# A state-space block and an attention block on one core: order of work around the second head pair, and a fourth padded buffer

## The reference, cut to what matters

```python
x = x + _L0_conv_ref(_gn(x), ...)          # block 0: selective scan
# block 1, on v = _gn(x)
qkv = einsum('bchw,oc->bohw', v, w_qkv) + b_qkv
qkv = conv3x3_depthwise(qkv, w_dw) + b_dw
q, k, v = split(qkv); q, k, v -> (b, 4 heads, 48, 2304)
q = q / max(sqrt(sum_channels(q * q)), 1e-12); k likewise
attn = softmax(einsum('bhdn,bhdm->bhnm', q, k) * temperature)
out = einsum('bhnm,bhdm->bhdn', attn, v)
x = x + einsum('bchw,oc->bohw', out, w_proj) + b_proj
```

## Time and profile before

| what | value |
|---|---|
| median of 3 runs | 15295.29 us |
| the profiled execution's own time | 15298.41 us |
| its span (first to last instruction) | 15296.6 us |
| mean granted clock of TensorE | 0.968 of full |
| TensorE matmul busy | 86% of the span |
| VectorE / ScalarE / GpSimd busy | 84% / 72% / 69% |

### The profile page before, as it was taken

How to read it: one execution, slowest core, us unless ns; L and a number is a source line. 1 busy time by engine, 2 the same in 40 slices (tenths; PEclk the granted TensorE clock), 3 DMA queues, 4 the chain that set the end, 5 groups by cost and what they waited for, 6 DMA issues and landing times.

```text
span 15296.6 us, 237874 instructions
## 1 busy us (share of the span) xinstructions
PE 13084.6 (86%) x60888; PEld 7840.4 (51%) x60888; DVE 12871.7 (84%) x13813; ACT 11081.7 (72%) x22746; POOL 10502.7 (69%) x4158
## 2 busy tenths in 40 slices
PE   6888888889888888888988889888898888988889
PEld 4555455554555545555455554555445554455544
DVE  8999669996799857998589984899849998499984
ACT  5887578875788657886578866788667886678865
POOL 6998069980699707997079960899608995099950
PEclk9999999999999999999999999999999999999999
DMA  3433023430334303342034420334203342044420
GB/s 111 129 129 114 20 93 129 138 96 20 97 129 138 92 20 103 129 138 87 20 111 129 136 80 20 115 129 136 75 20 120 129 135 71 20 129 129 132 65 25
DMA packets 907942, 1467.94 MB, mean 96 GB/s; under 512 B 38912, under 2 KB 891904, under 8 KB 893664
## 3 DMA queue, kind: packets, MB, share of 16 engines
q1 hardware_dynamic: 906560, 1452.37, 29.9%
HBM read 1350.07 MB, written 102.17 MB: 95 GB/s over the span
## 4 chain that ended last, share of the span: by engine, by line
PE 31%; issue 22%; POOL 19%; DVE 18%; ACT 5%; DMA 4%; DVEq 1%; ACTq 0%; POOLq 0%; SPq 0%
POOL area L1490 14%; DVE area L1013 13%; PE ps L838 9%; PE ps L849 8%; POOL area L1500 5%; PE ps L654 4%; DMA area<-bc_rows 4%; DVE area L1031 3%; ACT ps L1294 1%; PE ps L584 1%; PE ps L752 1%; PE ps L729 1%; PE ps L641 1%; ACT ps L1255 1%; PE ps L712 1%
## 5 line engine op out<-in xcount | busy, mean ns | idle before, releaser
L1013 DVE TENSOR_TENSOR_SCAN area<-ps,hst,area 128x384 f32<-128x384 f32 x9216 | 8571.3, 993 | 116.4 <-POOL area L1490 48.8
L1490 POOL TENSOR_TENSOR area<-area 128x1152 f32<-128x1152 f32 x3072 | 8001.9, 2638 | 50.3 <-POOL area L1479 38.1
L1294 ACT ACTIVATE ps<-area,a_neg 128x384 f32<-128x384 f32 x9216 | 5289.3, 580 | 1148.0 <-DVE area L1013 1087.8
L654 PE MATMUL ps<-area,ident 128*128 128x384 f32 x12672 | 4610.8, 501 | 790.4 <-POOL area L1500 722.0
L654 PEld LDWEIGHTS ps<-area,ident 128*128 128x128 f32 x12672 | 2277.6, 193 | 2506.5 <-POOL area L1500 947.2
L1474 POOL TENSOR_TENSOR area<-area,ones 128x2304 f32<-128x2304 f32 x8 | 43.3, 5417 | 3521.5 <-ACT area L1219 3399.9
L641 PE MATMUL ps<-ident,area 128*128 128x128 f32 x17280 | 2420.8, 277 | 5.2 <-ACT area L1263 5.2
L1433 ACT ACTIVATE area<-ps,t_neg,area 128x768 f32<-128x768 f32 x1728 | 1617.7, 986 | 984.6 <-PE ps L838 984.6
L641 PEld LDWEIGHTS ps<-ident,area 128*128 128x128 f32 x17280 | 2195.1, 193 | 58.9 <-ACT area L1263 9.5
L1500 POOL TENSOR_TENSOR area<-area 128x1152 f32<-128x1152 f32 x768 | 2024.8, 2636 | 34.7 <-ACT hst L1239 34.7
L1263 ACT ACTIVATE area<-ps,area 128x384 f32<-128x384 f32 x2880 | 1637.4, 569 | 535.1 <-PE ps L632 531.5
(11 more groups left out here) (128 smaller groups left out, 9606.7 us busy)
## 6 DMA issues: line engine op xcount, KB each, us to landing
area<-bc_rows SPq DMA_DIRECT2D x1536, 768.0 KB, 6.8
xz<-x_normed SPq DMA_DIRECT2D x144, 288.0 KB, 6.3
area<-in_x SPq DMA_DIRECT2D x18, 1728.0 KB, 10.4
area<-x_padded SPq DMA_DIRECT2D x24, 1250.0 KB, 5.6
z_raw<-z_st SPq DMA_DIRECT2D x144, 192.0 KB, 6.2
area<-z_raw SPq DMA_DIRECT2D x8, 3456.0 KB, 15.0
x_padded<-x_st SPq DMA_DIRECT2D x120, 200.0 KB, 7.7
x_normed<-area SPq DMA_DIRECT2D x9, 1728.0 KB, 7.9
```

The lines of the kernel that those rows point to most:

```text
L654: m = e.matmul(ps[:, 5 + j, 0:CH], ident[:], hb[:, i % NH, j], start=i == 0, stop=i == N - 1)
L1013: e.tensor_tensor_scan(rev(hb[:, i % NH, j], k), rev(ps[:, 2 + j, 0:CH], k), rev(dbu[:, i % NH, j], k), hst[:, i, j:j + 1], ALU.mult, ALU. ...
L1294: e.activation(ps[:, 2 + j, 0:CH], dlt[:, par, j], ACT.Exp, scale=a_neg[:, j, k, i:i + 1]).then_inc(da, 1)
L1490: e.tensor_tensor(dbu[:, i % NH], du[:, par], row_b[:, q % 2, i % ROWS:i % ROWS + 1].broadcast_to([128, J, CH]), ALU.mult).then_inc(dbus, 1)
```

## The change

- A fourth padded buffer: `xp2` gets `xpads[1]`, and `PAD_OF` says which buffer a tile takes: tiles 0 to 3 have one each, tile 4 reuses buffer 0, tile 5 buffer 1. `pad_qkv(i)` waits only for i > 3, and then for the convolution of tile i - 4. GpSimd clears the border of a fourth buffer: four more memsets for each image.
- In pair 0, `qkv(3)`, `qkv(4)` and `qkv(5)` each move one place ahead on PE and ACT: tile 3 before the transposes of v, tile 4 before the norms of q, tile 5 directly after them.
- `k_norms` is split in two halves of nine matmuls. In pair 1 the first half goes between `q_norm(1, 3)` and `q_norm(1, 4)`; in pair 0 the halves follow each other.
- On DVE, `scale_q(1)` and `newton_k(1)` go after two divisions of pair 0, ahead of the other four.
- On PE, the wait for six divisions moves from before the first `scores` of pair 1 to before its first `values`.

```diff
--- before.py
+++ after.py
@@ -93,6 +93,7 @@
 WQ = SUMS + 128
 WPR = WQ + CT * QT * 128
 XPAD2 = WPR + PAIRS * C + 4
+PAD_OF = (0, 1, 2, 3, 0, 1)
 UK = 3
 UC = UK * NC
 UNIT_AT = (10, 14)
@@ -194,7 +195,7 @@
         kz = ar(KZ, PAIRS * L).rearrange("p (i l) -> p i l", i=PAIRS)
         v_v = ar(V, PAIRS * L).rearrange("p (i l) -> p i l", i=PAIRS)
         vt = ar(VT, PAIRS * MT * 128).rearrange("p (i m c) -> p i m c", i=PAIRS, m=MT)
-        xp2 = [ar(XP2 + i * PADS, PAD).rearrange("p (h w) -> p h w", h=HP) for i in range(3)]
+        xp2 = [ar(XP2 + i * PADS, PAD).rearrange("p (h w) -> p h w", h=HP) for i in range(3)] + xpads[1:]
         kr = ar(KS, 2 * MT)
         kn = ar(KS + 2 * MT, PAIRS * 2 * MT).rearrange("p (i m) -> p i m", i=PAIRS)
         ksc = ar(KS + 6 * MT, PAIRS * 2 * MT).rearrange("p (i m) -> p i m", i=PAIRS)
@@ -346,7 +347,7 @@
         def conv_qkv(e, b, i):
             p, kind = divmod(i, 3)
             e.wait_ge(qk_ev, b * 36 + (6 * i + 6 + 2))
-            conv_taps(e, b * 108, i, cv2, xp2[i % 3], (v_v[:, p], q_v[:, p], kz[:, p])[kind], w_dw, b_dw)
+            conv_taps(e, b * 108, i, cv2, xp2[PAD_OF[i]], (v_v[:, p], q_v[:, p], kz[:, p])[kind], w_dw, b_dw)
 
         def copy_vt(e, b, p, g):
 
@@ -771,13 +772,14 @@
                     e.matmul(ps[:, c % 2, 0:CH], hones[:], sqq[p][:, c * CH:(c + 1) * CH],
                              start=True, stop=True).then_inc(n_mm, 1)
 
-                def k_norms(p):
+                def k_norms(p, half):
 
                     e.wait_ge(qsq, b * 4 + 2 * p + 2)
-                    for m in range(MT):
+                    for m in range(MT // 2 * half, MT // 2 * (half + 1)):
                         i = e.matmul(ps[:, 2, 2 * m:2 * m + 2], sqk[p][:, m * 128:(m + 1) * 128], hind[:],
                                      start=True, stop=True)
-                    i.then_inc(n_mm, 1)
+                    if half == 1:
+                        i.then_inc(n_mm, 1)
 
                 def row_sum(p, c):
 
@@ -790,15 +792,16 @@
                     if p == 0:
                         for i in range(3):
                             qkv(i)
+                        qkv(3)
                         wait_cv2(e, b, 0)
                         for g in range(5):
                             transpose_v(0, g)
-                        qkv(3)
+                        qkv(4)
                         for c in range(NC):
                             q_norm(0, c)
-                        qkv(4)
                         qkv(5)
-                        k_norms(0)
+                        k_norms(0, 0)
+                        k_norms(0, 1)
                         e.wait_ge(qk_ev, b * 36 + 36 + 2)
                     else:
                         e.wait_ge(ex, (b * 6 + 3) * 36 + 3)
@@ -810,8 +813,10 @@
                                 row_sum(0, 0)
                                 row_sum(0, 1)
                                 group_sum(b * 2 + 3, 1)
+                            if c == 4:
+                                k_norms(1, 0)
                             q_norm(1, c)
-                        k_norms(1)
+                        k_norms(1, 1)
                         row_sum(0, 2)
                         row_sum(0, 3)
                         wait_cv2(e, b, 3)
@@ -820,7 +825,6 @@
                         row_sum(0, 4)
                         row_sum(0, 5)
                         e.wait_ge(gn_v, b * 2 * GN_OPS + 4 * GN_OPS)
-                        e.wait_ge(on, b * 12 + 6)
                     e.wait_ge(vt_ev, b * 10 + (5 * p + 5))
                     e.wait_ge(qn, b * 2 + (p + 1))
                     e.wait_ge(k_ac, b * 6 + (3 * p + 3))
@@ -845,6 +849,9 @@
                             e.wait_ge(ex, base + (w + 4))
                             if w == 0:
                                 e.wait_ge(o_ev, turn + 1)
+                                if p == 1 and c == 0:
+                                    alone(e)
+                                    e.wait_ge(on, b * 12 + 6)
                             for s in range(2):
                                 i = e.matmul(ps[64 * h:64 * h + 64, 6 + s, 0:CH], vt[:, p, m, 64 * h:64 * h + 64],
                                              pb[:, w % 4, s * CH:(s + 1) * CH], start=m == 0, stop=m == MT - 1)
@@ -1122,10 +1129,12 @@
                 e.wait_ge(x_in, b * 32 + 64)
                 channel_stats(xf)
                 groupnorm(b * 2 + 3, 0, xf, xf)
-                for c in range(NC):
-                    divide(0, c)
+                divide(0, 0)
+                divide(0, 1)
                 scale_q(1)
                 newton_k(1)
+                for c in range(2, NC):
+                    divide(0, c)
                 e.wait_ge(n_mm, b * 14 + 14)
                 e.wait_ge(vt_mm, b * 10 + 10)
                 conv_tiles(b + 1)
@@ -1356,13 +1365,13 @@
 
                 def pad_qkv(i):
 
-                    if i >= 3:
-                        wait_cv2(e, b, i - 3)
+                    if i > 3:
+                        wait_cv2(e, b, i - 4)
                     alone(e)
                     with e.Fori(0, 3) as cc:
                         for s in range(2):
                             e.wait_ge(qk_mm, b * 36 + cc * 2 + (6 * i + s + 1))
-                            e.activation(xp2[i % 3][:, ds(cc * 16 + (8 * s + 1), 8), 1:1 + W],
+                            e.activation(xp2[PAD_OF[i]][:, ds(cc * 16 + (8 * s + 1), 8), 1:1 + W],
                                          ps[:, 6 + s, 0:CH].rearrange("p (h w) -> p h w", w=W),
                                          ACT.Identity, bias=b_qkv[:, i:i + 1]).then_inc(qk_ev, 1)
 
@@ -1397,14 +1406,14 @@
                     if p == 0:
                         for i in range(3):
                             pad_qkv(i)
+                        pad_qkv(3)
                         for g in range(5):
                             copy_vt(e, b, 0, g)
-                        pad_qkv(3)
+                        pad_qkv(4)
                         wait_cv2(e, b, 1)
                         e.activation(sqq[0], q_v[:, 0], ACT.Square).then_inc(qsq, 1)
                         for c in range(NC):
                             q_norm(0, c)
-                        pad_qkv(4)
                         pad_qkv(5)
                         k_norms(0)
                     else:
```

## The result

| kernel | median, us | runs |
|---|---|---|
| before | 15294.74 | 15293.58 to 15296.45 (4) |
| changed | 15188.81 | 15186.56 to 15191.55 (4) |

The ratio is 0.9931, 95% interval 0.9918 to 0.9944: 105.9 us faster, where 77 were forecast (15218). The time lies in the range, 4.8 us above its lower end. The profiled execution of the changed kernel has a span of 15187.3 us against 15296.6, and the mean granted clock went from 0.968 to 0.973.

A forecast was written before the change was run, and what follows sets the result against it. Attention's PE-ACT chain, its pair 1 scores held up by `scale_q`, was taken as what to relieve. 3.84 + 4.61 + 0.7 + 0.5 = 9.65 us an image, 77.2 for eight, gave 15218 us; range 15184 to 15250.

The forecast's parts named there:

- Norms in halves: Pair 1, PE: first nine norms of k fill the gap before `q_norm(1, 4)`, what follows moves forward; 3.84 us an image.
- `scale_q` ahead and the wait moved: Pair 1, DVE and PE: first scores no longer wait for `scale_q`, the divisions' wait moves to the values; 4.61 us an image.
- The divisions take it back: Rival, chance 0.13: pair 1's late root of k delays divisions, or the stop moves to the values; 40 us in all, 15255.
- the case of a full clock: Pair 1: were first scores at full clock, 1.4 us less, first values would still have half a microsecond to spare.
- The first scores: Pair 1, PE: first scores at 0.50 clock might run faster without the stop; bounds 0 and 3.1 us, 0.7 taken.
- Pair 0: Tiles one place ahead: norms of k start 3.65 us earlier but probably at half clock; between 0 and 3.65, 0.5 taken.
- HAM oscillation — how this bites in real kernels: Skill's rule: PE waiting between bursts starts the next cold; by it pair 0's term is 0, the kernel at 15222.
- The first rival: Chance 0.14: clock stays up for pair 0's norms and both pairs' first scores; 14.1 us an image, 113 in all, 15182.

The follow-up runs named there:

- scale_only: Kernel before with scale_q and newton_k behind two divisions and the divisions' wait moved to the first values, norms of k whole: 15223.85 us, ratio 0.9955.
- before_warm1: Kernel before with five 128x384 matmuls added on PE in pair 1, in the idle time ahead of the first scores, waits unchanged: 15272.02 us, ratio 0.9986.
- after_warm0: Changed kernel with six 128x384 matmuls added on PE in pair 0, behind tile 5 and ahead of the norms of k: 15180.77 us, ratio 0.9924.
- pad_only: Kernel before with only the fourth padded buffer and the new places of tiles 3 to 5: 15280.84 us, ratio 0.9991.
- wait_back_again: Changed kernel with the wait for six divisions back ahead of pair 1's first scores, measured once more: 15223.70 us, 15200.91 to 15241.44 in 12 executions.
- wait_back: Changed kernel with the wait for six divisions moved back ahead of pair 1's first scores: 15226.67 us, 15200.59 to 15235.58 in four executions.
- warm_mix0: Changed kernel with six matmuls added ahead of pair 0's norms of k and one more behind every fourth norm, four in all: 15209.74 us.

## Why the prediction was right, and where it was off

- **Norms in halves, 3.84 us: right.** 2.07 us for the first half in the gap, `q_norm(1, 4)` not delayed, 3.84 saved behind it. Alone it gave 24.5 us in place of 31 (3.1 an image; 3.5 by the length of attention).
- **`scale_q` ahead and the wait moved, 4.61 us: right.** Together with the halves 8.52 by the trace against 8.45. "The divisions take it back" did not happen: the values had 2.2 us to spare. The prediction had left half a microsecond for the case of a full clock; the last division ends about where it said, 1.9 us after the first score starts, but the values come later, since the second eight scores, which wait for an exponential, stand ahead of them (9353.07).
- **The first scores, 0.7 us: the term that was mis-sized.** It measured 3.42, beyond the bound of 3.1, and makes 22 us of the 29 that the forecast fell short. I had the bounds from the right rows and then took a value near the row of before, because PE "does little from 3716 on". That weighed the wrong stretch: scale_only has the slow norms in it and scores at full clock behind them, before_warm1 shows that filling the stop alone is enough. The edit removes the stop that lowered the clock, and with it the reason to stay near the row of before. The bound was low by 0.3 because I took the steady 2.94 us between the first pairs of exponentials; with a full clock the first two stand 9354.66 - 9352.02 = 2.64 apart.
- **Pair 0, 0.5 us: right in kind, slightly generous.** It measured between -0.2 and 0.4. The estimate from the earlier trace rows, 7.7 us of norms at half clock behind the idle time, came out as 7.84. The rule of "TensorE: Matmul & The Clock Gate", section "HAM oscillation — how this bites in real kernels", in the Trainium skill that spoke against this part held here: the clock fell in the idle time of 5.11 us, and the norms behind it ran at 0.50. It is not the whole cause: with that time down to 1.88 us in after_warm0 the norms of image 4 still took 7.61.
- **Not in the sum: the front of the next image, 1.69 us in six images, 10 us in all.** No edit touches it. With the 22 of the first scores, and 1 to 5 off for pair 0, it accounts for the 29 us to within 2. Why the clock fell there before and holds now, no run tells; image 1 of the changed kernel is still slow there, and pad_only, scale_only and wait_back_again show stretches that change sides in the same way between images and between executions. The range had room for this, the forecast had not; that part of the measured time's place in the range is luck.
- The first rival, the clock that stays up everywhere, gave the right size (113 us against 106) with the wrong place: it had 3.65 us in pair 0, and those stayed away. That its number came closer than the forecast's is luck.

## What to carry to other kernels

A stop of TensorE next to a dense stretch has two prices, the stop itself and the slow start behind it; here 4.6 and 3.4 us, and an edit that takes the stop away should be credited with both (a shorter stop, 2.4 us in wait_back, cost the second price in some executions only). Work brought forward on TensorE into idle surroundings, on the other hand, can run at half the clock and give back all that it gained: a buffer that let 36 small matmuls start 3.65 us earlier was worth nothing. Adding the parts' own times is no proof that each part works: the buffer alone measured 13 us, most of which lay in a stretch that it did not touch.

## What the runs showed of the hardware that I had not expected

- A stop of 2.43 us ahead of the scores leaves the clock up in one execution and brings it down in another, the same in seven images of either: 15200.59 against 15236.75 us for one kernel, of which the stop's clock is 2.7 us an image.
- Forty extra 128x384 matmuls made a kernel 22 us faster, ratio 0.9986 (0.9977 to 0.9996).
- TensorE can be busy without a gap and lose its clock: matmuls with two columns went from 1.05 to 1.71 us per eight rows in the middle of such a stretch (warm_mix0, image 4), and larger ones among them, which went from 0.89 to 1.63 us each, prevented it in four images of eight.
